# Own results ordered by a drain on VectorE and ScalarE, and one increment per group of running sums, in a two-layer graph network kernel

## The reference

```python
h = relu(layernorm(x))
m = relu(concat(h[src], edge_attr) @ W_msg.T + b_msg)      # one row per edge, 128 + 64 -> 128
m = relu(m @ W_msg2.T + b_msg2)
h_neigh = segment_sum(m, dst) / max(count(dst), 1)
x = x + concat(h, h_neigh) @ W_apply.T + b_apply           # first layer
h = relu(layernorm(x))
alpha = softmax of edge_weight over the edges of one destination
agg = project(segment_sum(alpha * h[src], dst))            # project(v) = v / (norm(v) + 1e-9)
comb = project(0.5 * (h @ W_self + b_self + agg @ W_nb + b_nb))
out = x + layernorm(comb) * gamma + beta                   # second layer
```

## Time and profile before

| | |
|---|---|
| median of 3 runs | 10865.57 us (10851.8 to 10873.19) |
| profiled execution, its own time | 10872.07 us |
| its span | 10870.3 us |
| PE busy | 5331.9 us (49%) |
| DVE busy | 3580.0 us (33%) |
| ACT busy | 1136.7 us (10%) |
| POOL busy | 6155.9 us (57%) |
| mean granted clock of PE | 0.669 of full speed |
| DMA | 618.8 MB, 57 GB/s |

### The profile page before, as it was taken

The page is one execution under the profiler, slowest core; times in us unless marked ns, Lnnn a source line. Parts: engine busy times, 40 slices in busy tenths (PEclk is TensorE's granted clock), DMA queues, the critical chain, the costliest instruction groups (busy, mean ns, idle before and its releaser), DMA issues.

```text
span 10870.3 us, 94616 instructions
## 1 busy us (share of the span) xinstructions
PE 5331.9 (49%) x26549; PEld 4117.8 (38%) x26549; DVE 3580.0 (33%) x14159; ACT 1136.7 (10%) x2108; POOL 6155.9 (57%) x6486
## 2 busy tenths in 40 slices
PE   4666666666655555566666533332333233233334
PEld 3444444444444344344444423222222222222224
DVE  4333233323222222222222433333333333333336
ACT  2111111111111111111111200000000000000002
POOL 4555555555554444455555466666666666666663
PEclk7777777777777677777777655655555555555556
DMA  4222222222222222222222222221111111111112
GB/s 151 56 57 54 56 56 55 57 58 57 61 67 56 57 57 59 58 55 56 58 56 57 65 57 56 56 55 49 46 46 47 46 46 47 46 46 47 46 47 72
DMA packets 412673, 618.83 MB, mean 57 GB/s; under 512 B 171795, under 2 KB 274175, under 8 KB 411263
## 3 DMA queue, kind: packets, MB, share of 16 engines
q0 software_dynamic: 206336, 422.99, 15.0%
q1 hardware_dynamic: 192624, 183.30, 6.1%
q10 hardware_dynamic: 13200, 6.56, 0.2%
HBM read 576.45 MB, written 35.92 MB: 56 GB/s over the span
## 4 chain that ended last, share of the span: by engine, by line
another core or an unknown queue 49%; PE 25%; issue 12%; DVE 12%; ACT 1%; DVEq 1%; DMA 0%; SPq 0%; POOL 0%; ACTq 0%; POOLq 0%
PE bank L1056 13%; DVE acc L884 7%; PE bank L1118 6%; PE bank L1115 3%; PE bank L1053 2%; DVE onehot L887 1%; DVE work L887 1%; ACT work L581 1%; DVEq L866 1%; DVEq L884 0%; DVE xq L711 0%; DVE acc L711 0%; DVE acc L995 0%; ACT work L587 0%
## 5 line engine op out<-in xcount | busy, mean ns | idle before, releaser
L493 POOL DMA_INDIRECT rows_ring<-p_table,idx x3224 | 3087.5, 958 | 2951.8 <-DMA idx<-in_src_ring 1790.9
L884 DVE TENSOR_TENSOR acc<-acc,bank 128x128 f32 x6448 | 1826.0, 283 | 7192.7 <-remote 5639.5
L493 POOL DMA_INDIRECT rows_ring<-h_table,idx x3224 | 3052.5, 947 | 1635.2 <-issue 1013.2
L887 DVE TENSOR_SCALAR onehot<-iota,dloc,coef 128x128 f32<-128x128 f32 x4840 | 1703.6, 355 | 16.5 <-ACT coef L558 13.3
L1056 PE MATMUL bank<-work,rows_ring 128*128 128x128 f32 x3216 | 694.6, 370 | 1867.6 <-DVE work L887 665.6
L1056 PE MATMUL bank<-onehot,work 128*128 128x128 f32 x6448 | 1094.4, 325 | 863.4 <-issue 676.4
L1056 PE MATMUL bank<-onehot,rows_ring 128*128 128x128 f32 x3232 | 743.8, 401 | 1247.1 <-remote 594.9
L1056 PEld LDWEIGHTS bank<-work,rows_ring 128*128 128x128 f32 x3216 | 597.9, 270 | 1968.7 <-issue 1911.4
L1056 PEld LDWEIGHTS bank<-onehot,work 128*128 128x128 f32 x6448 | 1002.8, 237 | 898.9 <-issue 711.3
L1056 PEld LDWEIGHTS bank<-onehot,rows_ring 128*128 128x128 f32 x3232 | 651.6, 297 | 1323.7 <-issue 1261.4
L1118 PE MATMUL bank<-work,we_sb 64*128 64x512 f32 x1612 | 1045.4, 724 | 164.7 <-issue 164.1
(11 more groups left out here) (121 smaller groups left out, 1066.1 us busy)
## 6 DMA issues: line engine op xcount, KB each, us to landing
work<-in_edge_t SPq DMA_DIRECT2D x403, 256.0 KB
rows_ring<-p_table,idx POOLq DMA_INDIRECT x3224
rows_ring<-h_table,idx POOLq DMA_INDIRECT x3224
idx<-in_src_ring SPq DMA_DIRECT2D x404, 8.0 KB
ht_rows<-rows_ring SPq DMA_DIRECT2D x25, 256.0 KB, 2.3
p_table<-rows_ring SPq DMA_DIRECT2D x25, 256.0 KB, 2.5
work<-ht_rows SPq DMA_DIRECT2D x25, 256.0 KB
h_table<-work ACTq DMA_DIRECT2D x25, 256.0 KB
```

What stands on the lines that cost most here:

```text
L493: pool.indirect_dma_start(out=rows_ring[:, 16 * h + G * k + j, :], out_offset=None, in_=table[:, :], in_offset=bass.IndirectOffsetOnAxis(a ...
L884: dve.tensor_tensor(win, win, ps_sum[layer][k % slots][:, j * P:(j + 1) * P], ALU.add).then_inc(added, 1)
L887: ins = dve.tensor_scalar(hot_slots[layer][k % slots][:, j * P:(j + 1) * P], iota[:, :], dloc[:, ds(t, 1)], coef[:, ds(t, 1)], ALU.is_equa ...
```

## The change

Semaphores `vector_order`, `scalar_order` and `inverse_order` and the class `Order` go. `link` becomes a drain of DVE: the next instruction is held until what was issued before has completed. Marks and waits of DVE's tail step become drains at the places of the waits; ACT's pair of activations (L652) gets a drain. In `sums_and_onehots` DVE drains before each of the four sums, also before the first, and only the fourth sum increments `added`, once per group. What waits for `added` counts groups, and FINAL is rounded up to groups.

```diff
-FINAL = [min(T, (E - N + (c + 1) * G * P - 1) // P + 1) for c in range(NBATCH)]
-X1_AT = -(-FINAL[0] // G) + 3
+FINAL = [-(-min(T, (E - N + (c + 1) * G * P - 1) // P + 1) // G) for c in range(NBATCH)]
+X1_AT = FINAL[0] + 3
...
-                    order.link(act.activation(four_of(sc_b, c), four_of(sc_b, c), ACT.Sqrt))
+                    act.activation(four_of(sc_b, c), four_of(sc_b, c), ACT.Sqrt)
+                    act.drain()
...
-            order = Order(dve, S["vector_order"])
-            link = order.link
+
+            def link(ins):
+
+                dve.drain()
...
                 for j in range(G):
                     if adds:
-                        if later(gs * G + j):
-                            dve.wait_ge(added, gs * G + j)
+                        dve.drain()
                         win = acc[:, ds(at[j], P)]
-                        dve.tensor_tensor(win, win, ps_sum[layer][k % slots][:, j * P:(j + 1) * P], ALU.add).then_inc(added, 1)
+                        total = dve.tensor_tensor(win, win, ps_sum[layer][k % slots][:, j * P:(j + 1) * P], ALU.add)
                     if hots:
...
+                if adds:
+                    total.then_inc(added, 1)
                 if hots:
                     ins.then_inc(hot, 1)
...
-                inverse.link(dve.reciprocal(coef[:, a:z], coef[:, a:z]))
+                link(dve.reciprocal(coef[:, a:z], coef[:, a:z]))
...
                 if inv is not None:
-                    order.after(marks["inv"])
-                    marks["inv"] = order.mark(dve.reciprocal(root, root))
+                    dve.drain()
+                    dve.reciprocal(root, root)
                 if raw is not None:
...
-                    order.after(marks["stats", raw])
-                    marks["diff"] = order.mark(dve.tensor_tensor(diff, me, mo, ALU.subtract))
+                    dve.drain()
+                    dve.tensor_tensor(diff, me, mo, ALU.subtract)
...
-                            pe.wait_ge(S["sums0_added"], 4 * g - 4)
+                            pe.wait_ge(S["sums0_added"], g - 1)
...
-                            pe.wait_ge(S["sums1_added"], 4 * g - 12)
+                            pe.wait_ge(S["sums1_added"], g - 3)
```

More of the change, by code:

```diff
@@ L169, in gnn @@
         names = """weights_loaded counts_in_loaded soft_in_loaded tile_arrays_loaded pad_zeroed constants_made
-            vector_order pool_order pool_turns vector_turns
-            rows_loaded bias_ready var0_ready root0_ready scale0_ready fourth0_ready limits0_made inverse_order normed0_ready normed0_turned ht0_ready p_in_psum p_ready
+            pool_order pool_turns vector_turns
+            rows_loaded bias_ready var0_ready root0_ready scale0_ready fourth0_ready limits0_made normed0_ready normed0_turned ht0_ready p_in_psum p_ready
             ends_ready ends_turned ends_read carry_ready carry_turned carry_read
@@ L179, in gnn @@
             squares_ready norms_in_psum norm_root_ready nb_in_psum u_ready
-            scalar_order unit_arg_ready unit_root_ready var2_ready root2_ready scale2_ready rows2_ready scaled_ready fin_ready""".split()
+            unit_arg_ready unit_root_ready var2_ready root2_ready scale2_ready rows2_ready scaled_ready fin_ready""".split()
         S = {n: sem(n) for n in names}
@@ L254, in live @@
             return not isinstance(i, int) or 0 <= 8 * i + k - lag < NG
[L256 to L285, removed]
         CHUNKS1 = [*(range(c, c + 2) for c in range(0, 20, 2)), *(range(c, c + 1) for c in range(20, NBATCH))]
@@ L633, in four_of @@
                 return arr[:, c * G:(c + 1) * G]
-            order = Order(act, S["scalar_order"])
             def tail_step(s):
@@ L935, in _ @@
             inverse_cuts = [0, *range(128, T, 194)]
-            inverse = Order(dve, S["inverse_order"])
             def invert_counts(n):
                 a, z = inverse_cuts[n], (*inverse_cuts[1:], T)[n]
-                inverse.link(dve.reciprocal(coef[:, a:z], coef[:, a:z]))
+                link(dve.reciprocal(coef[:, a:z], coef[:, a:z]))
             between = {n: lambda n=n: invert_counts(n) for n in range(1, len(inverse_cuts))}
@@ L949, in four_of @@
                 return arr[:, c * G:(c + 1) * G]
-            marks = {}
             def tail_step(s):
@@ L962, in tail_step @@
                     dve.wait_ge(S["norm_root_ready"], inv + 1)
-                    marks["inv"] = order.mark(dve.tensor_scalar(root, root, NORM_EPS, None, ALU.add))
+                    dve.tensor_scalar(root, root, NORM_EPS, None, ALU.add)
                 if fin_c is not None:
@@ L975, in tail_step @@
                     mu, v, r2 = four_of(mean, raw), four_of(var, raw), four_of(sc_b, raw)
-                    order.after(marks["stats", raw])
-                    marks["diff"] = order.mark(dve.tensor_tensor(diff, me, mo, ALU.subtract))
-                    marks["parts"] = order.mark(dve.tensor_tensor(both_parts, se, so, ALU.add))
-                    marks["mu"] = order.mark(dve.tensor_tensor(mu, me, mo, ALU.add))
+                    dve.drain()
+                    dve.tensor_tensor(diff, me, mo, ALU.subtract)
+                    dve.tensor_tensor(both_parts, se, so, ALU.add)
+                    dve.tensor_tensor(mu, me, mo, ALU.add)
                 if gam is not None:
@@ L984, in tail_step @@
                 if raw is not None:
-                    order.after(marks["mu"])
-                    marks["v"] = order.mark(dve.scalar_tensor_tensor(v, diff, P / 4.0, diff, ALU.mult, ALU.mult))
-                    marks["r2"] = order.mark(dve.scalar_tensor_tensor(r2, mu, P / 4.0, mu, ALU.mult, ALU.mult))
+                    dve.drain()
+                    dve.scalar_tensor_tensor(v, diff, P / 4.0, diff, ALU.mult, ALU.mult)
+                    dve.scalar_tensor_tensor(r2, mu, P / 4.0, mu, ALU.mult, ALU.mult)
                 if inv is not None:
                     c = inv
-                    order.after(marks["inv"])
+                    dve.drain()
                     dve.wait_ge(S["nb_in_psum"], c + 1)
@@ L998, in tail_step @@
                 if raw is not None:
-                    order.after(marks["r2"])
-                    marks["v"] = order.mark(dve.tensor_tensor(v, v, both_parts, ALU.add))
+                    dve.drain()
+                    dve.tensor_tensor(v, v, both_parts, ALU.add)
                 stats = batch_at(3)
@@ L1005, in tail_step @@
                         ins = dve.bn_stats(stat6[:, at, :], acc[:, at * P:(at + 1) * P])
-                    marks["stats", stats] = order.mark(ins)
                 if raw is not None:
-                    order.after(marks["v"])
+                    dve.drain()
                     dve.tensor_tensor(r2, r2, v, ALU.add).then_inc(S["unit_arg_ready"], 1)
@@ L1012, in tail_step @@
                     dve.wait_ge(S["root2_ready"], scl + 1)
-                    marks["scale"] = order.mark(dve.reciprocal(scale, scale))
+                    dve.reciprocal(scale, scale)
                 if arg is not None:
@@ L1018, in tail_step @@
                 if scl is not None:
-                    order.after(marks["scale"])
+                    dve.drain()
                     dve.scalar_tensor_tensor(mu_s, mu_s, -0.5, scale, ALU.mult, ALU.mult).then_inc(S["scale2_ready"], 1)
```

## The result

The changed kernel took 11007.8 us (median of 4), the kernel before 10860.9 beside it: a ratio of 1.0142, with an interval of 1.0116 to 1.0168. I had forecast 10,460 and a range up to 10,950. The profiled execution of the changed kernel took 11046.2 us.

What follows compares the result with a forecast made beforehand. Bound: increments sent while gathers run get through late, making POOL stand 2571 us. Terms -205 - 232 + 33 = -404 us from the median 10865.6 gave 10461, called 10460; range 10,050 to 10,950, forecast's own 10,110 to 10,800.

Steps and rivals of the forecast that it cites:

- In proportion to all traffic, 5950 x 3.4% = 205 us: First layer: 12 of 348 increments per half body go, so the stretch shortens by 205 us.
- its twin of 232 us for the second layer: Second layer: 3 of 75 increments per group go; gain taken as the middle of 187 and 277 us.
- if lateness depends on the gathers alone, nothing is won: First layer's lower bound: leaving out increments gains nothing.
- The increment called 27 us late: Second layer: increment of PE's product ending at 8485.86, read as reaching DVE's step of 8513.47 27 us late.
- the stand that ended at 4687.92: First layer: POOL's 7.60 us stand, read as an index load queued behind SP's edge loads awaiting PE's product.
- The pace of 0.72 us: DVE's running sums: with drains one every 0.72 us, a group 2.9 us in place of 1.9.
- I price this at nothing between the ends: DVE's longer group step costs nothing in the layers: 7192.7 us idle, and 2.9 under the gathers' 5.0 us.
- my slower rival: Second layer, behind POOL's restarts: DVE's longer step adds POOL stops; 11,060 to 11,225 us, chance 0.14.
- The tail: Last 97 us: drains in some 19 closing steps, five with sums, make it 33 us dearer, between 10 and 50.
- the range's low end: Low end of the forecast's own bounds: 10866 - 802 + 50 = 10,114 us.
- Links and ScalarE: Scans and inverses swap waits for drains at 0 +- 5 us; ScalarE's 25 tail drains are hidden by DVE.
- POOL behind the index load: First layer: index load queued behind SP's edge loads, POOL restarting after 7.60 us; no gain was assigned.

Runs made afterwards that it cites:

- index_first: Kernel before, with SP's first-layer index load for a half body issued ahead of the edge loads of the half before it: 0.9186, 9969.9 us.
- links_only: Kernel before, with only the links of scans, row statistics and inverses and the one of ScalarE's tail as drains: 1.0009.
- extra_incs: Kernel before, with three more increments a group: the first three one-hots increment a semaphore that nobody reads: 1.0008.
- tail_drains: Kernel before, with drains in VectorE's tail steps alone, marked operations keeping their increments: 1.0031.
- drains_layer1: Kernel before, with drains in place of VectorE's own waits in the second layer's running sums alone, all increments kept: 1.0036.
- drain_four_incs_2: Changed kernel with all four sums of a group incrementing again and drains kept, timed again on the third group's chip: 1.0155 of before.
- drains_layer0: Kernel before, with drains in place of VectorE's own waits in the first layer's running sums alone, all increments kept: 1.0100.
- drain_behind_sum: Kernel before with the sums' part alone, each drain moved right behind its sum, ahead of the one-hot; one increment a group: 1.0112.
- hold_for_onehot: Kernel before, no drains added; each sum also waits for the one-hot ahead of it, by a semaphore the one-hots increment: 1.0150.
- first group's chip: Chip that timed extra_wait, rest_only, sums_only and drain_four_incs beside the kernel before, which took 10774.9 us there.
- extra_wait: Kernel before, with one more VectorE wait ahead of each sum, on a semaphore already at its value: 1.0006.
- rest_only: Changed kernel with its running sums put back to own waits and four increments; scans, inverses, tail and ScalarE keep drains: 1.0042 of before.
- sums_only: Kernel before with the running sums' part alone: a drain ahead of each sum, one increment per group, waits in groups: 1.0066.
- drain_four_incs: Changed kernel with each of the four sums incrementing again, readers counting tiles, drains kept: 1.0102 of before.

## Why the prediction was wrong

**The bound was read right as far as POOL's standing goes, and wrong as to what feeds it.** I read the late increments as sent by the engines and held up by the gathers, and gave each increment left out a share of the layer's time, in proportion to all traffic. The step that failed is "In proportion to all traffic, 5950 x 3.4% = 205 us", with its twin of 232 us for the second layer. The runs show nothing in its place: three more increments a group gave 1.0008 [0.9995, 1.0022], and drains with four increments or with one gave 1.0155 and 1.0154 to 1.0156, on different chips. The traces fit this. In the first layer of before, DVE's first step after a stop of POOL starts 3.0 us after it (mean of 76 stands of over 2 us ahead of a body's first half) and 3.4 us (98 ahead of its second); with three more increments a group it is 3.0 and 3.45, in the changed kernel 3.4 and 3.4 (3.3 and 3.4, 3.0 and 3.5 in its other two traces). So I read it that the gathers' stop releases what is held, whatever number of increments is under way. My own lower bound, "if lateness depends on the gathers alone, nothing is won", was the true case, and the rule of the Trainium skill (VectorE: DVE Perf Modes, The DRAIN you can't avoid), by which the semaphores after each operation cost nothing, agrees with these runs as far as the increments go (1.0008). A prompt own wait was also the better ordering of the two: it lets the sum start while the one-hot runs, as at 8487.23 in the earlier trace rows, 0.09 us before the one-hot's end.

Two readings were too strong. The increment called 27 us late: DVE ran the step before until 8498.60 and asked for it only then, so it was late by the 14.88 us of the earlier trace rows at least, and by 27 at most. And the label of the stand that ended at 4687.92 names PE's product, not the index load, which SP issued at 4684.15; that the queue counts is shown by index_first, not by that row.

**The drains were priced right and then hidden wrongly.** The pace of 0.72 us came as 0.70. The step that failed is "I price this at nothing between the ends", whose cover was that DVE has idle time and that a group's 2.9 us are under the 5.0 of its gathers. That is an average. What the runs showed in its place: 1.0100 for the drains in the first layer's sums, 1.0036 for those in the second's, and 1.0150 for the same holding without any drain. A stand of the first layer in the changed kernel, ACT, DVE, SP and POOL in order of time (DVE's rows are the first sums of three groups):
```profile
3142.99 0.60 ACT L549 ACTIVATE work<-bank 128x512 f32<-128x512 f32 x1 [17.70 <-remote]
```
```profile
3141.68 0.29 DVE L853 TENSOR_TENSOR acc<-acc,bank 128x128 f32 x1 [35.33 <-remote]
...
3144.49 0.29 DVE L853 TENSOR_TENSOR acc<-acc,bank 128x128 f32 x1 [0.17 <-issue]
...
3147.85 0.29 DVE L853 TENSOR_TENSOR acc<-acc,bank 128x128 f32 x1 [0.70 <-PE bank L1023]
```
```profile
3143.25 10.60 SPq L347 DMA_DIRECT2D work<-in_edge_t  x2
3154.02 0.47 SPq L319 DMA_DIRECT2D idx<-in_src_ring  x1
```
```profile
3157.81 0.94 POOL L461 DMA_INDIRECT rows_ring<-p_table,idx  x1 [20.48 <-DMA idx<-in_src_ring]
```
Work comes in bursts: everything waits, is released at once, and PE, ACT and DVE then work off the groups in turn while POOL stands. DVE does two steps back to back, and each takes 2.8 us in place of 1.9. This is the mechanism of my slower rival, one place away: I had it in the second layer, with 200 to 360 us, and the larger part sits in the first.

How the longer step comes to lengthen POOL's stands is argued, and only in part counted. PE's products with the edge features (L1118 in before) can be counted by whether they end in one of POOL's some 174 stands of over 2 us. On three chips and in the first pair of traces it was 219 to 225 of 806 in the kernels without held sums (before, links_only, extra_incs, tail_drains, drains_layer1), and 236 to 254 in those with them (the three traces of the changed kernel, drain_four_incs_2, drains_layer0, drain_behind_sum, hold_for_onehot). The rate in the stands is near the same, 0.114 to 0.124 products a us, so the 12 more of drains_layer0 are about 100 us, and 69 to 80 were measured. On the first group's chip the count says otherwise: 217 and 207 without held sums (extra_wait, rest_only), 202 and 206 with them (sums_only, drain_four_incs), at a lower rate in the latter (0.106 and 0.108 in place of 0.118 and 0.111), though the stands are 41 to 66 us longer there as well. What holds in all sixteen traces is that DVE ends fewer of its 806 steps in the stands: 350 to 403 with held sums, 418 to 432 without. (The two kernels with the index load moved are not in these counts.) Such counts tell where the work went, not why.

One rival for the path stands untested: PE's clock. Between the stands of the first layer its granted clock was 0.78 in every kernel without held sums and 0.76 to 0.77 in those with them, while in the stands it was 0.64 to 0.65 in all. On the first group's chip, where the sums cost least (1.0066), it did not fall (0.78 to 0.79). A slower PE while POOL gathers would leave more products for the stands; no run holds the clock and changes the step, so which of the two leads is open. That holding the sums is what starts it is shown, by hold_for_onehot and drains_layer0 with extra_incs and extra_wait beside them. No single wait of PE for DVE's sums or one-hots shows the path: they come to 9 us in the first layer of before and 12 in hold_for_onehot. But some 700 us ahead of PE's products in either are labelled "issue", and a wait that the profile doesn't name could be among them.

**Second layer.** Predicted -232, measured +26 here and +32 to +40 in the traces of the second to the fourth group. With the drains there alone it is 27 to 32, so on that chip they are the cost. POOL's standing rose from 645 to 671 us. I had no term for it. What stays open is why hold_for_onehot and drain_behind_sum, with a like pace and with the clock at 0.51 and 0.52, keep 4663 and 4659 us there, and why the changed sums lost nothing there on the first group's chip (4653 and 4652, against 4660 in extra_wait). PE's lower clock goes with the held sums in all of them, and so is not what costs the stretch its 30 us.

**The tail** was +33 predicted, +32 in the traces; with its drains alone 1.0031. The price of a full step without sums held: 3.95 us became 5.2, the 1.3 predicted. That the total fits is part luck: behind the last gather of before there are 24 steps, not 19, and eight of them have sums, not five. Those eight got 1.7 to 2.7 us longer each, and the last eight are short ones that got under 0.8 longer, where I had all 19 at 1.3. At the range's low end the sum also adds the dear tail (50) where the cheap one (10) belongs: 10,074 and not 10,114, which changes nothing. **Links and ScalarE**, at 0 +- 5 us, measured 1.0009 [0.9997, 1.0022], which can't be told from nothing.

**POOL behind the index load**, which I had named and not used, was the larger lever by far: 900 us in one edit of the order of two loads. index_first is the best version found, 8.1% under before; the change costs it 1.1% of before too, so it is best without the change.

## What to carry to other kernels

- An engine that is idle for two thirds of the span is no cover for a slower step of it, if its work comes in bursts behind a release. Look at what follows the longest waits, step by step, and ask whether the longer operation stands there.
- A wait on one's own earlier increment orders only what it names; a drain orders everything ahead of it. Where independent work is put between two dependent operations, as the one-hots here, the drain gives that overlap away.
- Before counting what an event costs, see what ends the waits: where many of them end together at one event (here the gathers' stop), fewer messages may change nothing, and the order in the queue that the stopped engine waits for can be worth more.
- Time the parts of a change on the chip that times the whole. A count that carries the explanation has to be made for every trace at hand, also those on the chip where the effect is small.

## What the runs showed of the hardware

- While POOL gathers without a pause, DVE's sums can come 2.8 us apart with nothing awaited, with drains (8485.14 to 8487.94, a drain and a register instruction of 0.70 us each between them) and without (8489.56 to 8492.42 in before). One more satisfied wait per sum cost nothing over the run (1.0006), which speaks for this slowness being mostly off the path; its cause is open.
- PE's granted clock in the second layer fell from 0.58 to 0.51 or 0.52 in each kernel whose sums are held there, by drains or by a semaphore, and stayed at 0.58 in each whose are not. What PE did before: the same products, but started by one-hots that come 0.63 to 0.74 us apart in place of 0.46. PE's busy time there grew by 240 us from 1491; hold_for_onehot has the same growth (1723) in a stretch of 4663 us, so the gathers hide it.
- Chips differ in what the same edit costs: the drains with four increments gave 1.0102 on the first group's chip and 1.0155 on the third's, with intervals that do not touch.
